# Attention batch by batch, with the first batch's norm, routing and scatter among the second batch's heads

## What is computed

```python
x = _layernorm(x + _L0_attn_ref(...))   # 16 heads of 64, q and k normalized, softmax over the batch's 1024 keys
x = _layernorm(x + _L0_ffn_ref(...))    # 8 experts of 512, the two best of a token, silu(gate) * up, down
x = _layernorm(x + _L1_attn_ref(...))   # depthwise convolution of width 3, state recurrence of 16 states
x = _layernorm(x + _L1_ffn_ref(...))    # 8 experts, the two best of a token, relu squared, and a shared expert
```

## Time and profile before

| what | value |
|---|---|
| runs shown | 1081.29, 1078.69 and 1076.44 us, median 1078.69 |
| the profiled execution's own time | 1075.24 us |
| its span | 1073.5 us, 1.7 us less than its time |
| granted clock of PE, mean | 0.925 of full speed (2.4 GHz) |
| attention, to its last addition | 626.1 us from the span's start |
| first tile of phase 0 | 674.9 us |
| between the last addition and the first tile | 48.7 us, PE busy 12.0 us of it |

### The profile page before, as it was taken

How to read it: one execution, slowest core, us unless ns; L and a number is a source line. 1 busy time by engine, 2 the same in 40 slices (tenths; PEclk the granted TensorE clock), 3 DMA queues, 4 the chain that set the end, 5 groups by cost and what they waited for, 6 DMA issues and landing times. The chain is left out here.

```text
span 1073.5 us, 34731 instructions
## 1 busy us (share of the span) xinstructions
PE 913.9 (85%) x13676; PEld 858.4 (80%) x13676; DVE 728.1 (68%) x1463; ACT 770.0 (72%) x1275; POOL 501.1 (47%) x385
## 2 busy tenths in 40 slices
PE   4889999999999999999999951899969469899930
PEld 2778998999989989989999841899969359899830
DVE  6699988988998898889888744432459669410202
ACT  5689998988999889989988640544464266598831
POOL 5475755564655555555646116512328152043433
PEclk8799999999999999999999965899999689899975
DMA  8300000000000000000000041313201002023211
GB/s 263 113 2 6 18 3 22 3 3 22 3 3 22 3 22 3 3 23 3 2 22 2 2 177 38 103 54 86 54 26 30 3 28 70 11 68 97 61 55 42
DMA packets 43131, 42.13 MB, mean 39 GB/s; under 512 B 5600, under 2 KB 37344, under 8 KB 42848
## 3 DMA queue, kind: packets, MB, share of 16 engines
q1 hardware_dynamic: 38880, 31.51, 9.6%
q0 software_dynamic: 4096, 8.40, 2.7%
HBM read 25.60 MB, written 14.29 MB: 37 GB/s over the span
## 5 line engine op out<-in xcount | busy, mean ns | idle before, releaser
L557 ACT ACTIVATE Pr<-SC,cur_nesc,cur_esc 128x1024 f32<-128x1024 f32 x256 | 309.9, 1211 | 33.5 <-PE SC L417 17.0
L654 DVE TENSOR_TENSOR Pl<-Pr 128x1024 f16<-128x1024 f32 x224 | 287.5, 1302 | 44.8 <-ACT Pr L557 43.0
L416 PE MATMUL SC<-QK 128*128 128x256 f16 x1024 | 238.7, 274 | 1.0 <-ACT QK L539 1.0
L417 PE MATMUL SC<-QK 128*128 128x256 f16 x1024 | 238.6, 273 | 0.0
L442 PE MATMUL OP<-V,Pr 128*128 128x65 f16 x2048 | 214.4, 192 | 5.8 <-DVE Ob L676 5.7
L444 PE MATMUL OP<-V,Pr 128*128 128x64 f16 x2048 | 215.2, 195 | 0.0
L446 PE MATMUL OP<-V,Pl 128*128 128x65 f16 x2048 | 214.0, 191 | 0.0
L442 PEld LDWEIGHTS OP<-V,Pr 128*128 128x128 bf16 x2048 | 191.0, 97 | 12.5 <-issue 8.2
L444 PEld LDWEIGHTS OP<-V,Pr 128*128 128x128 bf16 x2048 | 190.0, 97 | 2.5
L446 PEld LDWEIGHTS OP<-V,Pl 128*128 128x128 f16 x2048 | 190.7, 99 | 0.0
L789 POOL TENSOR_TENSOR stk<-nrm,stk 128x512 f16<-128x512 f32 x64 | 75.2, 1175 | 147.6 <-DVE stk L636 147.6
(11 more groups left out here) (191 smaller groups left out, 2178.8 us busy)
## 6 DMA issues: line engine op xcount, KB each, us to landing
ys<-yb SPq DMA_DIRECT2D x92, 64.0 KB, 1.5
xg<-xs SPq DMA_DIRECT2D x12, 384.0 KB, 4.4
wst<-in_up SPq DMA_DIRECT2D x8, 512.0 KB, 3.5
xs<-zero SPq DMA_DIRECT2D x2, 1472.0 KB, 13.1
scratch<-in_up SPq DMA_DIRECT2D x1, 2304.0 KB, 8.2
wd<-in_wd SPq DMA_DIRECT2D x4, 576.0 KB, 10.7
wd<-in_wd SPq DMA_DIRECT2D x4, 512.0 KB
QK<-in_wqkv SPq DMA_DIRECT2D x4, 384.0 KB, 7.2
```

What stands on the lines that cost most here:

```text
L416: eng.matmul(out, QK[:, b, 1, key:key + P], rhs, start=True, stop=False)
L417: mm = eng.matmul(out, QK[:, b, 2, key:key + P], rhs, start=False, stop=True)
L557: eng.activation(Pr[:, n % PB, :, :], SC[s % 2][:, :, :], ACT.Exp, bias=cur_nesc[:, b:b + 1], scale=cur_esc[:, b:b + 1]).then_inc(s_exps, 1)
L654: eng.tensor_tensor(Pl[:, n % PB, :, :].rearrange("p a b -> p (a b)"), pr, high(pr)[:, 1::2], ALU.subtract).then_inc(s_low_probs, 1)
```

## The change

Attention's loop keeps its pairs and slots, but the 16 "heads" of the loop are now: 0 to 7 all of batch 0, 8 to 15 all of batch 1, each of them two real heads of one batch (`token_tile`, `head_of`). So batch 0's attention output is complete when pair 4 ends. In pairs 5, 6 and 7 (`NORM_I`, `CHOOSE_I`, `PLACE_I`) the first batch's norm, turning, logits, choice, ranks, places and its 16 scatters stand one by one at slots; where a value lies in bank M1 (turned x, logits, ranks), PE waits at the head of slot 22 (pairs 5 and 6) or slot 3 (pair 7), ahead of that slot's scores, until it has been read. The second batch's norm stands before the loop of tiles and at its first tiles, its routing at tiles 2 to 10, its scatter after that. The second block starts with the load of batch 0's sorted rows. The loads of phase 1 stand behind the stores of tiles 19 to 22 (before: 14 to 22), and `load_offsets(1)` is cut into four, at tiles 23, 29, 35 and 41. The weights' copies of the second layer (`w1_high`, `w1_low`) move from tiles 0 to 7 to tiles 13 to 20. The scales of the exponentials are read from full tables, so two small DVE operations a head are gone. `Constants`' POOL operations move from the tail to pair 2. The mixing weights of phase 1 (`probabilities(1)`, three small DVE operations, behind `weights(1)`, one of ACT) move behind phase 1, ahead of `step_inputs(0)`.

```diff
+TB = NT // B
+TILES = 23
+NORM_I, CHOOSE_I, PLACE_I = 5, 6, 7
+EARLY_TURN_AT = (18, 21)
+EARLY_LOGITS_AT = (16, 17, 18, 19)
+CONSTANTS_I = 2
+CONSTANTS_AT = (2, 3, 9, 11, 12, 14, 18)
+SCATTER_AT = 14
...
+        def token_tile(h, v):
+
+            return TB * (h // TB) + v % TB
+
+        def head_of(h, v):
+
+            return 2 * (h % TB) + v // TB
...
+            def early(i, s):
+
+                h, sh = 2 * i + s // SLOTS, s % SLOTS
+                tp = before(tp_slot, sh + 1)
+                if i == NORM_I and s in EARLY_TURN_AT:
+                    n = EARLY_TURN_AT.index(s)
+                    m1_free(h + 1, tp, i, s, 1)
+                    eng.wait_ge(s_rows, 4 * n + 4)
+                    wait(eng, s_xT, n)
+                    for r in range(4):
+                        mm = eng.transpose(M1[:, P * r:P * r + P], t["x"][:, 4 * n + r, :], ident32[:, :])
+                    mm.then_inc(s_x_turned, 1)
+                if i == CHOOSE_I and s in EARLY_LOGITS_AT:
+                    n = EARLY_LOGITS_AT.index(s)
+                    if n == 0:
+                        m1_free(h + 1, tp, i, s, 1)
+                        eng.wait_ge(s_xT, 2)
+                        eng.wait_ge(constants.s_loaded, 16 * 9)
+                    for k in (2 * n, 2 * n + 1):
+                        mm = eng.matmul(M1[:, E * k:E * k + E], xT0[k // 4][:, P * (k % 4):P * (k % 4) + P], t["gate"][:, :], start=True,
+                                        stop=True)
+                    mm.then_inc(s_logits, 1)
+                if (i, s) == (PLACE_I, 1):
+                    m1_free(h + 1, tp, i, s, 1)
+                    eng.wait_ge(s_mask, 1)
+                    eng.wait_ge(constants.s_made, 7)
+                    mask, n = t["mask"][:, 0, :], (TB + 1) * E
+                    eng.matmul(M1[:, 0:n], t["tri16"][:, :], mask, start=True, stop=False, skip_group_check=True)
+                    for k in range(1, TB + 1):
+                        mm = eng.matmul(M1[:, E * k:n], t["ones16"][:, :], mask[:, 0:n - E * k], start=False,
+                                        stop=k == TB, skip_group_check=True)
+                    mm.then_inc(s_ranks, 1)
 
             def slot(i, s):
+                if (i, s) == (NORM_I, 22):
+                    eng.wait_ge(s_xT, 2)
+                if (i, s) == (CHOOSE_I, 22):
+                    eng.wait_ge(s_logits_read, 1)
+                if (i, s) == (PLACE_I, 3):
+                    eng.wait_ge(s_ranks_read, 1)
...
+            def early(i, s):
+                if i == NORM_I and 13 <= s < 13 + TB:
+                    k = s - 13
+                    eng.wait_ge(s_nmr, 1)
+                    xk = t["x"][:, k, :]
+                    eng.activation(xk, xk, ACT.Identity, bias=nmr[:, k:k + 1], scale=rstd[:, k:k + 1]).then_inc(
+                        s_rows, 1)
+                if i == NORM_I and s in EARLY_TURN_AT:
+                    n = EARLY_TURN_AT.index(s)
+                    eng.wait_ge(s_x_turned, n + 1)
+                    eng.activation(xT0[n], M1[:, :], ACT.Copy).then_inc(s_xT, 1)
+                if (i, s) == (NORM_I, 28):
+                    eng.wait_ge(s_rows, TB)
+                    eng.activation(split[:, :, 0:D], t["x"][:, 0:TB, :], ACT.Copy).then_inc(s_split_high, 1)
+                if (i, s) == (CHOOSE_I, 30):
+                    eng.wait_ge(s_differences, 1)
+                    eng.activation(ex[:, :], df[:, :], ACT.Exp).then_inc(s_exp, 1)
...
+            def early_norm(s):
+
+                if s < TB:
+
+                    wait(eng, s_out_added, 8 * (H // 2 // B))
+                    eng.bn_stats(stats[:, s, :], t["x"][:, s, :]).then_inc(s_stats, 1)
+                if 1 <= s <= TB:
+                    eng.wait_ge(s_stats, s)
+                    eng.bn_aggr(mv[:, s - 1, :], stats[:, s - 1, :]).then_inc(s_mv, 1)
+                if s == TB + 1:
+                    eng.wait_ge(s_mv, TB)
+                    eng.tensor_scalar(ve[:, :], mv[:, :, 1], EPS, None, ALU.add).then_inc(s_ve, 1)
+                if s == TB + 4:
+                    eng.wait_ge(s_rstd, 1)
+                    eng.scalar_tensor_tensor(out=nmr[:, :], in0=mv[:, :, 0], scalar=-1.0, in1=rstd[:, :],
+                                             op0=ALU.mult, op1=ALU.mult).then_inc(s_nmr, 1)
+                if s == 29:
+                    eng.wait_ge(s_split_high, 1)
+                    eng.tensor_tensor(split[:, :, D:2 * D], t["x"][:, 0:TB, :], split[:, :, 0:D],
+                                      ALU.subtract).then_inc(s_split_low, 1)
...
+            def early_choose(s):
+
+                if s == 20:
+                    eng.wait_ge(s_logits, len(EARLY_LOGITS_AT))
+                    eng.tensor_copy(lg[:, :, :], M1[:, 0:TB * E].rearrange("p (k e) -> p k e", e=E)).then_inc(
+                        s_logits_read, 1)
...
+                if s == 2:
+                    eng.wait_ge(s_ranks, 1)
+                    eng.tensor_copy(rank[:, :, :], M1[:, 0:(TB + 1) * E].rearrange("p (k e) -> p k e", e=E)).then_inc(
+                        s_ranks_read, 1)
...
+                if i == PLACE_I and SCATTER_AT <= s < SCATTER_AT + 2 * TB:
+                    m = s - SCATTER_AT
+                    if m == 0:
+                        eng.wait_ge(s_slots, 1)
+                        eng.wait_ge(s_split_low, 1)
+                        eng.wait_ge(constants.s_cleared, 16 * B)
+                    eng.indirect_dma_start(
+                        out=t["xs"][0],
+                        out_offset=bass.IndirectOffsetOnAxis(ap=t["slots"][:, 0, m // TB, m % TB:m % TB + 1], axis=0),
+                        in_=split[:, m % TB, :], in_offset=None).then_inc(s_scattered, 16)
...
+ROWS_0, TURN_0, LOGITS_0, CHOOSE_0, RANKS_0, PLACE_0 = 0, 2, 3, 5, 9, 9
+LOW_AT = 13
...
-                if j in (14, 17, 20):
-                    load(1, (j - 14) // 3)
+                if j in (19, 20, 21):
+                    load(1, j - 19)
...
-                    if ph == 3 and j % CHUNK == 0:
+                    if ph in (1, 3) and j % CHUNK == 0:
...
-            turn(0, 0)
-            logits(0)
-            turn(0, 1)
-            logits(1)
-            ranks(0)
-            ranks(1)
             load_offsets(0)
-            load_offsets(1)
             sorted_turn(0)
             for u in range(SHARED_0 + LAG2):
                 if u + 1 < SHARED_0:
@@ -1213,6 +1456,13 @@
                     up_products(u)
                 if u >= LAG2:
                     down_products(u - LAG2)
+                if u == TURN_0:
+                    turn(0, 1)
+                if u in (LOGITS_0, LOGITS_0 + 1):
+                    at = 4 * (u - LOGITS_0)
+                    logits(1, range(at, at + 4))
+                if u == RANKS_0:
+                    ranks(1)
...
-                if u < 2 * NC:
-                    w1_high(u)
+                if u in (ROWS_0, ROWS_0 + 1):
+                    rows(0, 1, (u - ROWS_0,))
+                if u == TURN_0:
+                    read(0, 1)
+                if u == TURN_0 + 1:
+                    split_high(1)
+                if LOW_AT <= u < LOW_AT + 2 * NC:
+                    w1_high(u - LOW_AT)
...
             sigmoids(0)
+            weights(1)
...
             convolve(0)
+            probabilities(1)
             step_inputs(0)
...
-            inverse_deviations(0, 0)
             inverse_deviations(0, 1)
-            scatter(0)
-            scatter(1, -3)
+            scatter(1)
             gather(0, 25)
```

More of the change, by code:

```diff
@@ L298, in attention @@
         constants = Constants(nc, t, io, sb, sem)
+        xT0 = [half_of[:, 0:S].bitcast(F32) for half_of in (xT_hi, xT_lo)]
+        split = sb("split0", [P, TB, 2 * D], F16)
+        stats = sb("stats0", [P, TB, 6], F32)
+        mv = sb("mv0", [P, TB, 2], F32)
+        ve, rstd, nmr = (sb(n, [P, TB], F32) for n in ("ve0", "rstd0", "nmr0"))
+        lg = sb("lg0", [P, TB, E], F32)
+        mx = sb("mx0", [P, TB, 8], F32)
+        ix = sb("ix0", [P, TB, 8], U32)
+        ixf = sb("ixf0", [P, 2, TB], F32)
+        df, ex, e1 = (sb(n, [P, TB], F32) for n in ("df0", "ex0", "e10"))
+        hot = sb("hot0", [P, 2, TB, E], F32)
+        rank = sb("rank0", [P, TB + 1, E], F32)
+        over = sb("over0", [P, E, E], F32)
+        tiles, cum, base = (sb(n, [P, E], F32) for n in ("tiles0", "cum0", "base0"))
+        pos = sb("pos0", [P, TB, E], F32)
+        prod = sb("prod0", [P, 2, TB, E], F32)
+        slot_values = sb("slot_values0", [P, 2, TB], F32)
+        past = sb("past0", [1, TILES, E], F32)
+        owner = sb("owner0", [1, TILES], F32)
+        (s_stats, s_mv, s_ve, s_rstd, s_nmr, s_rows, s_x_turned, s_xT, s_split_high, s_split_low) = (
+            sem("early_" + n) for n in ("stats", "mv", "ve", "rstd", "nmr", "rows", "turned", "xT", "split_high",
+                                        "split_low"))
+        (s_logits, s_logits_read, s_largest, s_differences, s_indices, s_index_values, s_one_hot, s_mask, s_exp,
```

(22 more changed lines are left out.)

305 lines of the change are left out of this document (209 added, 96 removed).

## The result

The changed kernel took 1105.26 us (median; 1104.3 to 1105.79) against 1079.54 (1076.44 to 1081.29) before, a median that includes a fourth execution: a ratio of 1.0245, interval 1.0218 to 1.0272. I had forecast 1072.8. Its profiled execution, which I call the record run, has a span of 1103.0 us, 29.5 more than before.

A forecast was written before the change was run, and what follows sets the result against it. PE was taken to bound attention and tiles, so only the 48.7 us between the blocks could win; the terms summed to −5.9, from 1075.24 to 1069.3, or 1072.8 by the median; own range 1067 to 1078, whole range 1063 to 1082.

The forecast's parts named there:

- barrier to first tile: Between the blocks: batch 0's rows load needs only the barrier and SP's queue; first tile earlier, −33.1 us (31.7 to 33.9).
- pair 5: Attention: PE's turns and wait at slot 22, ACT's rows and reads, and the split add 5.5 us (1.1 to 8.2).
- pair 6: Attention: the logits' matmuls and slot 22's wait for their copy add 4.5 us (1.4 to 5.5).
- pair 7 and the rest of attention, to the barrier: Slot 3's wait for the ranks' copy adds 2.5 us (0.4 to 3.5).
- tiles 0 to 45: Batch 1's PE work +3.0, first phase 1 load's stall +4.0, its slower clock +1.7, load_offsets(1) +5.2: 13.9 us.
- behind them: Ahead of the scans: phase 1's mixing weights, three small DVE operations, add 0.8 us.
- The sixteen scatters on POOL: Pair 7, slots 14 to 29: taken as hidden, since POOL has 25.3 us left, 1.58 for each scatter.
- The gap: Between barrier and first tile: the weights ahead in SP's queue hold up batch 0's rows; first chunk lands about 641.8.
- fourth rival: Between the blocks: weights don't hold up the rows, first chunk lands at 632.8; 9.0 us more gain, 1063.8; chance 0.06.
- stall before tile 23: Among the tiles: phase 1's first load, behind tile 19's store, stalls PE by 4.0 us (3.1 to 5.7).
- third rival: Pair 7: scatters pace it, POOL's low half behind them; at 2.18 each +9.6 us, 1082.4; chance 0.12.
- rule of the Trainium skill: POOL and DVE share a locked port pair, so pair 7's scatters would be as slow as beside the scans, 2.18 each.

The follow-up runs named there:

- r1: The changed kernel run again with nothing edited: 1072.38 us, ratio 0.9966 to the kernel before.
- e4: e1 with the four loads of batch 0's sorted rows ahead of the second layer's weights in SP's queue: 1060.79 us, ratio 0.9858.
- e5: The changed kernel with only the four loads of batch 0's sorted rows moved ahead of the weights in SP's queue: 1062.92 us, ratio 0.9865.
- e6: The changed kernel with PE's three waits on bank M1 moved behind that slot's scores and products with V: 1103.73 us, ratio 1.023.
- e1: The changed kernel with waits meant to space POOL's scatters in pair 7 and among phase 0's tiles: 1073.76 us, ratio 0.9978.
- e2: The changed kernel with waits meant to space only the scatters among phase 0's tiles: 1073.34 us, ratio 0.9973.

## Why the prediction was wrong

Against the span before, in us; r1 is the same program without the crawl:

| term | predicted | record run | r1 |
|---|---|---|---|
| barrier to first tile (47.8 before) | −33.1 | −31.8 | −32.2 |
| pair 5 | +5.5 | +2.7 | +2.7 |
| pair 6 | +4.5 | +3.5 | +3.4 |
| pair 7 and the rest of attention, to the barrier | +2.5 | +18.5 | +8.7 |
| tiles 0 to 45 | +13.9 | +35.6 | +13.2 |
| behind them | +0.8 | +1.1 | +1.3 |
| sum | −5.9 | +29.5 | −2.9 |

**The step that failed** is the handling of the scatters, put at nothing: "The sixteen scatters on POOL, slots 14 to 29, I take as hidden", and, for batch 1, only the date of its last scatter was counted. In the earlier trace rows I asked whether POOL has the time, and what DVE does to POOL. What it costs PE, ACT and DVE when POOL issues back to back wasn't asked. The change itself took the distance away: before, `scatter(1, -3)` waited for a tile's gate products each time, which the diff shows as a removed line, and `scatter(0)` ran while PE was idle. The table's difference between record run and r1, 9.8 in attention and 22.4 in the tiles, is the crawl with the slow clock behind it (tile 15 takes 4.1 us at a granted clock of 0.55).

**The gap** was right: the queue holds the rows up, and the fourth rival (weights don't hold them up) is refuted by e4 and e5, where only the order changes and 10.7 us between barrier and first tile go.

**Pairs 5 and 6** were right in kind. The waits stand where they were computed, as these rows of the record run show (pairs 5, 6 and 7, and the stall before tile 23):

```profile
452.55 0.28 PE L468 MATMUL SC<-QK 128*128 128x256 f16 x1 [1.41 <-ACT xT_lo L666]
...
528.63 0.28 PE L468 MATMUL SC<-QK 128*128 128x256 f16 x1 [2.67 <-DVE lg L840]
...
561.90 0.28 PE L468 MATMUL SC<-QK 128*128 128x256 f16 x1 [2.37 <-DVE rank L876]
...
749.72 0.39 PE L1349 MATMUL XB<-ident,xg 128*128 128x128 f16 x2 [4.06 <-DMA xg<-xs]
```

Predicted were 1.5, 2.85, 2.5 and 4.0. Pair 5 was put too high (5.5 against 2.7), in two terms. For ACT's rows and the split 2.75 was added; PE's timeline in r1 has one wait by them, 0.80 us (437.13, behind the row that waits for nmr), and none at the split's slot. And the sum took PE's work and waits whole, without the 1.4 us in which PE had been idle before: in r1 PE is busy 0.9 longer in pair 5 and idle 1.7 longer (3.1 against 1.4), about the 2.7. In pair 6 it is 1.4 and 2.1. e6 shows the same from the other side: taking the waits away gave half of them.

**Pair 7** was put too low even in r1. Its own 5.65 (67.65 against 62.00) are the 2.4 of the ranks, 1.6 at slot 20, where PE waits for a low half that stood behind scatters on POOL (the third rival's mechanism), and 1.7 of smaller delays. The scatters took 0.95 to 2.27 beside the low halves, and slot 31's low half came late. POOL's timeline and PE's wait in r1:

```profile
618.11 1.83 POOL L1038 DMA_INDIRECT xs<-split,slots  x1 [0.30 <-issue]
620.25 1.83 POOL L1038 DMA_INDIRECT xs<-split,slots  x1 [0.30 <-issue]
...
626.93 0.20 PE L494 MATMUL OP<-V,Pr 128*128 128x65 f16 x1 [1.80 <-POOL Pl L992]
```

So the rule of the Trainium skill weighed in the prediction (page "SBUF — State Buffer", section "SBUF: two separate sides") agrees with these rows (1.83, against 0.96 alone). But the price was 1.6 us in the pair and, with the 1.80 above, some of the 3 more in the tail, where the clock granted is 0.75 (before 0.90), and not 9.6. **Among the tiles** 13.9 stands against 13.2. r1's 1072.38 beside 1072.8 is therefore in part luck: its span fell by 2.9, half of the 5.9.

## What to carry to other kernels

When a burst of POOL's indirect DMAs moves beside a busy PE, keep the waits that hold them apart, or put some in: in the groups with the crawl, phase 1's scatters 1.26 us apart cost PE 1.0 to 1.2 us for each, 1.8 us apart on average nothing. Ask of each moved instruction what it does to engines with which it shares no semaphore. And run the same kernel in more than one group before believing a difference: e1 and e2 seemed to prove a fix that hadn't been made, until r1 ran without it.

## What the hardware showed unexpectedly

PE can be slowed by scatters with which it shares neither data nor a semaphore: to 29 matmuls in 19.7 us instead of 276. ACT and DVE are held up with it, ACT first: it takes up one result of PE 3.7 us and the next 19 us later than in r1. It happened in the record run and in three of the five groups, there in every run that had bursts, and in no run of the other two. A burst of sixteen costs 17 to 19 us at tile 14, one of eight 8, one of 32 about 38. **Open** is what differs between the groups (the chip, or where program and tensors lie; since each group had a chip of its own, the runs can't separate the two), and the path by which POOL's scatters slow the other engines: the traces show neither. Among the tiles no distance between 1.26 and a mean of 1.8 us was tried, and gathers were not spaced on purpose.
